# One exponent a head pair, queries and keys in a PSUM bank each, and new instruction orders in a fused attention and feed-forward kernel

## The chip, the cores and the metric

The kernel runs on one core of a Trainium2 chip. The metric is the device time of one execution in microseconds. The kernel before takes 2145.38 us, the median of three runs (2141.57 to 2145.68).

A core has TensorE (PE), which multiplies matrices and writes PSUM; VectorE (DVE) and ScalarE (ACT), which read PSUM and SBUF; GpSimd (POOL), which here works in SBUF alone; and SyncE (SP), whose queue issues all DMAs. Each engine takes its instructions strictly in the order of its own queue and waits for others by semaphores. PSUM has eight banks of 128 x 512 float32.

## The reference

Sixteen sequences of 512 tokens with 128 channels go through two stages.

```python
h = layernorm(x) * (1 + ca) + sa
x = x + ga * latent_attention(h)          # 16 heads of 8, causal
h = layernorm(x) * (1 + cb) + sb
x = x + gb * two_layers(h)                # DEPTH = 2
# one of the two layers:
h = shift_token(x); q, k, v = split(h @ wqkv)      # 8 heads of 64
q, k = l2norm(q) * q_scale, l2norm(k) * k_scale    # per token and head
q, k = rotary_xpos(q, k)                           # cos and sin factors
sim = mask(8 * q @ k.T)      # windows of 64 tokens, own and previous window
x = x + (softmax(sim) @ v) @ wo
h = layernorm(shift_token(x)) * lg + lb
x = x + (a * gelu(g)) @ w2 + b2, where a, g = split(h @ w1 + b1)
```

All arithmetic of the local attention is in float32.

## The kernel before

A batch is one sequence. A sequence of 512 tokens is four tiles of 128. For every batch `steps()` (line 56) lists the named steps: the first attention (`max`, `rows1`, `score`, `ctx`, `turn`, `join`, `out`, in four groups of four heads), then per layer four tiles of `qkv`, `rotate`, `v`, `norm`, `qheads`, `kheads`, four head pairs of `wscore`, `wexp`, `share`, `pturn`, `wctx`, then `wout`, the normalisation (`center`, `spread`, `scale`) and the feed-forward (`hid`, `down`). At the end comes `final`.

Two streams, the even and the odd batches, share the engines, each with buffers of its own (S2 = 2). The order of each engine is written out. `PLACES` says in which order an engine takes the steps of one batch, and `TURNS` has a bit for each step of the merged queue that says which stream is next (`merged`, line 144). Before the change both streams use one list. `FIRST_BANKS` (line 161) names the PSUM bank of every tile that PE writes; PE waits until the readers of the bank's last tile are done (`Banks.take`, line 221). `FILLS` (line 187) puts filler matmuls in front of chosen tiles (line 234); their results are overwritten.

The part that changes is the layers' attention:

- `qkv` (line 586): PE multiplies queries and keys of a tile into two adjoining banks, 128x1024. ScalarE squares all of it (788). `rotate`: VectorE multiplies it by the cosine factors (982) and, in two halves of every head, by the sine factors (989), and reduces the squares to sums a head (991). GpSimd adds the two products (1091).
- `norm`: ScalarE takes Ln and Exp of the sums (798, 800) for the inverse norms, GpSimd clips them (1096) and multiplies the keys by theirs (1101). The queries stay unscaled.
- `qheads`, `kheads`: PE turns the tile (430) and ScalarE copies it from PSUM (805). The queries' turn waits for GpSimd's sum, that of the keys for the product.
- `wscore`: PE writes the band mask and the scores of a pair of heads into two banks (627, 636). VectorE takes the negated maximum of each row (1000) and multiplies it by the inverse norm of the query (1006).
- `wexp` (815): for each head of the pair and each tile one ScalarE exponent of 128x128, with the inverse norm as scale, the maximum as bias and the row's sum from the accumulator. That is eight exponents a pair, and eight accumulator reads.
- `share`: VectorE takes the reciprocal of the sums (1021), GpSimd multiplies the probabilities by them (1108). `pturn`: PE turns them, VectorE copies them out of PSUM (1014). `wctx`: PE multiplies by the values (658), ScalarE copies (821).

Line 777 is the exponent of the first attention, 947 and 942 its maxima, 449 and 445 its scores and masks on PE, 928 the normalised input of the feed-forward and 678 its first product, 1033 the gated hidden rows, 741 the Exp of the normalisation, 1155 the store of a batch.

Of the kernel before, what the change touches and what calls it, by code (L numbers as in the profile page):

```python
# [54 lines left out]
def steps():  # L55
# [3 lines left out]
    out = [("keep",), ("values",)] + units[0] + [("rows1", 0)] + units[1] + [("rows1", 1)]  # L59
# [8 lines left out]
    for l in range(DEPTH):  # L68
        for t in range(NT + 2):
            out += [("qkv", l, t), ("rotate", l, t), ("v", l, t)] * (t < NT) + [("norm", l, t - 1)] * (1 <= t <= NT)  # L70
            out += [("qheads", l, t - 2), ("kheads", l, t - 2)] * (t >= 2)
        for p in range(NP2 + 2):
            out += [("wscore", l, p), ("wexp", l, p, 0), ("share", l, p, 0), ("wexp", l, p, 1), ("share", l, p, 1)] * (p < NP2)
# [4 lines left out]
    cut = out.index(("qkv", DEPTH - 1, 0)) + 1  # L78
    first = {("kheads", DEPTH - 1, 2): [("stats", 0)], ("kheads", DEPTH - 1, 3): [("plain", 0)],
             ("wscore", DEPTH - 1, 0): [("load",)], ("wscore", DEPTH - 1, 1): [("proj", 0), ("proj", 1)]}  # L80
    between = []
    for last in out[cut:]:
        between += [(1, last)] + [(0, name) for name in first.get(last, [])]
    return between + [(0, name) for name in out[:cut]]

# [14 lines left out]
    "ACT": [  # L100
# [141 lines left out]
def build(nc, x, wdkv, wuk, wuv, wuq, wo1, wqkv, q_scale, k_scale, wo, ln_g, ln_b, w1, b1, w2, b2,  # L242
          cond, wmod, c_f32, c_bits, c_rot, c_edge, out):
    with ExitStack() as ctx:
# [180 lines left out]
        with nc.Block() as block:  # L425
# [420 lines left out]
            def _(dve):  # L846
# [6 lines left out]
                def step(b, kind, *a):  # L853
# [115 lines left out]
                    elif kind == "rotate":  # L969
# [14 lines left out]
                        if n:  # L984
                            dve.wait_ge(*sum_r.at(b, n))
# [256 lines left out]
```

## Time and profile before

| | before |
|---|---|
| median of the runs | 2145.38 us |
| span of the profiled execution | 2140.7 us |
| PE busy | 1949.1 us, 91% |
| ACT busy | 1607.3 us, 75% |
| DVE busy | 1559.3 us, 73% |
| POOL busy | 862.1 us, 40% |
| mean granted clock of PE | 0.989 |

The profile is of one execution. Its own time is told by its span, from the first to the last instruction, 2140.7 us; the runs are timed from outside, so the median stands 4.7 us above it. "Busy" is time in which an engine had at least one instruction under way. The matmuls' ends are modelled, so a share of 91% is not 91% of the peak. A group of instructions is named by line, engine, operation and tiles; in the tiles' names `ps` is PSUM, `pr` and `scr` are work space, `Q` and `Kf` the turned queries and keys. "Idle before" is time in which the engine stood still ahead of such an instruction, with the engine and line that ended it.

### The profile page before, as it was taken

To read this page: it belongs to the slowest core of one execution; us is meant where nothing else is said; L and a number is where in the kernel's file an instruction comes from. 1 tells how busy PE (TensorE), PEld (TensorE's weight loads), DVE (VectorE), ACT (ScalarE), POOL (GpSimd) and SP (SyncE) were. 2 spreads that over 40 slices of the span, in tenths; PEclk is the share of its full clock that TensorE was granted. 3 is DMA by queue.
4 is the path that set the end of the run, shared out by engine and by line. 5 is a ranking of instruction groups with operands and counts; after the bars stand their busy time and mean duration, and the time that the engine had idled before them with its cause. 6 is when DMAs were issued, how large, how long until landed. Compare 5 with 4: busy or idle time off the path is not lost.

```text
span 2140.7 us, 56185 instructions
## 1 busy us (share of the span) xinstructions
PE 1949.1 (91%) x22308; PEld 1117.7 (52%) x22308; DVE 1559.3 (73%) x2671; ACT 1607.3 (75%) x3975; POOL 862.1 (40%) x826
## 2 busy tenths in 40 slices
PE   6789999999999999999999999999999999999987
PEld 3344545555454655545555554655545455554644
DVE  3476787877778777787877778687777877777753
ACT  1567878787887878777787887878688787877755
POOL 2043616245351624526163361625435162452522
PEclk8999999999999999999999999999999999999999
DMA  4110201213030120202112030120203012030100
GB/s 137 29 32 16 61 7 36 41 24 58 7 68 9 39 43 24 58 7 57 21 32 51 24 58 7 38 39 24 58 7 70 13 36 42 24 53 7 36 6 23
DMA packets 63110, 76.19 MB, mean 36 GB/s; under 512 B 10630, under 2 KB 57856, under 8 KB 60800
## 3 DMA queue, kind: packets, MB, share of 16 engines
q1 hardware_dynamic: 62852, 72.60, 16.1%
q8 instruction: 180, 2.95, 0.6%
q14 instruction: 78, 0.64, 0.1%
HBM read 9.14 MB, written 4.19 MB: 6 GB/s over the span
## 4 chain that ended last, share of the span: by engine, by line
PE 56%; ACT 23%; DVE 12%; issue 5%; SPq 2%; DMA 1%; POOL 1%; DVEq 0%; ACTq 0%; POOLq 0%
PE ps L430 10%; ACT pr L815 6%; PE ps L667 5%; PE ps L564 5%; ACT pr L777 5%; PE ps L594 4%; PE ps L595 4%; PE ps L604 4%; PE ps L658 3%; PE ps L449 3%; ACT pr L788 3%; DVE wm L1000 3%; PE ps L678 2%; PE ps L445 2%; PE ps L687 2%
## 5 line engine op out<-in xcount | busy, mean ns | idle before, releaser
L1091 POOL TENSOR_TENSOR pr<-pr 128x1024 f32<-128x1024 f32 x128 | 302.2, 2361 | 739.7 <-DVE pr L989 739.7
L815 ACT ACTIVATE pr<-ps,wb,inv 128x128 f32<-128x128 f32 x768 | 340.8, 481 | 24.6 <-DVE wb L1006 24.2
L777 ACT ACTIVATE pr<-ps 128x1024 f32<-128x1024 f32 x320 | 314.4, 1028 | 42.5 <-PE ps L449 42.0
L1108 POOL TENSOR_TENSOR pr<-pr,shares 128x512 f32<-128x512 f32 x192 | 199.9, 1048 | 314.0 <-DVE shares L1021 314.0
L947 DVE TENSOR_REDUCE nm<-ps 128x2 f32<-128x256 f32 (+2 forms) x384 | 314.5, 861 | 13.0 <-PE ps L449 11.9
L430 PE MATMUL ps<-cf,pr 128*128 128x128 f32 x1792 | 259.7, 282 | 31.1 <-POOL pr L1108 22.5
L430 PEld LDWEIGHTS ps<-cf,pr 128*128 128x128 f32 x1792 | 200.9, 142 | 124.4 <-issue 55.0
L982 DVE TENSOR_TENSOR pr<-ps,rot 128x1024 f32<-128x1024 f32 x128 | 156.2, 1221 | 120.1 <-ACT pr L788 97.7
L788 ACT ACTIVATE pr<-ps 128x1024 f32<-128x1024 f32 x128 | 131.2, 1025 | 104.6 <-PE ps L595 66.2
L445 PE MATMUL ps<-cb 64*64 64x256 bf16 (+1 forms) x2560 | 175.3, 263 | 30.1 <-ACT pr L777 14.4
L1014 DVE COPY pr<-ps 128x512 f32<-128x512 f32 x256 | 170.1, 679 | 15.2 <-PE ps L430 13.7
L815 ACT ACTIVATION_READ_ACCUMULATOR pr<-ps,wb,inv 128x1 f32 x768 | 175.9, 229 | 0.0
L1000 DVE TENSOR_REDUCE wm<-ps 128x8 f32<-128x1024 f32 x128 | 155.6, 1216 | 25.9 <-PE ps L636 25.9
L989 DVE TENSOR_TENSOR pr<-ps,rot 128x512 f32<-128x512 f32 x256 | 163.7, 681 | 0.0
L445 PEld LDWEIGHTS ps<-cb 64*64 64x64 bf16 x2560 | 72.4, 104 | 168.5 <-issue 82.7
L564 PE MATMUL ps<-pr,V 128*16 128x512 f32 (+3 forms) x2048 | 152.4, 439 | 6.3 <-ACT pr L777 6.3
L991 DVE TENSOR_REDUCE scr<-pr 128x16 f32<-128x1024 f32 x128 | 154.8, 1209 | 0.0
L594 PE MATMUL ps<-Wqkv,hs 128*128 128x512 f32 x256 | 137.1, 617 | 7.4 <-ACT pr L777 3.6
L1101 POOL TENSOR_TENSOR pr<-pr,inv 128x512 f32<-128x512 f32 x128 | 133.4, 1042 | 19.3 <-POOL inv L1096 0.4
L636 PE MATMUL ps<-Kf,Q 64*64 64x128 f32 (+1 forms) x4096 | 137.0, 263 | 0.0
L658 PE MATMUL ps<-pr 128*64 128x64 f32 x2048 | 133.4, 229 | 2.1 <-DVE pr L1014 1.9
L636 PEld LDWEIGHTS ps<-Kf,Q 64*64 64x64 f32 x4096 | 129.7, 133 | 4.5
(158 smaller groups left out, 4040.0 us busy)
## 6 DMA issues: line engine op xcount, KB each, us to landing
pr<-V SPq DMA_DIRECT2D x32, 512.0 KB, 4.5
queries<-early SPq DMA_DIRECT2D x224, 64.0 KB
keys<-early SPq DMA_DIRECT2D x224, 64.0 KB
pr<-V SPq DMA_DIRECT2D x32, 384.0 KB, 6.6
xn<-in_L_attn_x SPq DMA_DIRECT2D x16, 256.0 KB, 4.5
out<-hT SPq DMA_DIRECT2D x16, 256.0 KB, 2.2
queries<-mT SPq DMA_DIRECT2D x128, 4.0 KB
Wqkv<-in_L_ffn_wqkv SPq DMA_DIRECT2D x1, 1536.0 KB
```

What stands on the lines that cost most here:

```text
L430: mm = pe.transpose(dst[:, t * P:(t + 1) * P], src(t), ident)
L445: pe.matmul(dst, identb[here, here], mask, start=True, stop=False, skip_group_check=True)
L564: mm = pe.matmul(bank[32 * j:32 * j + 16, kt * P:T], V1[s][:, kt, 4 * g + j, :], pr[s][:, j, OFF[kt]:OFF[kt] + T - kt * P], start=(kt == 0 ...
L594: pe.matmul(bank[:, 0:T], lhs, Wqkv[:, l, 0:T], start=True, stop=True)
L636: mm = pe.matmul(bank[D2 * half:D2 * half + D2, r * T + (t + 1) * P - wd:r * T + (t + 1) * P], Q2[s][rows, p, q0:q0 + D2], K2[s][rows, p, ...
L658: mm = pe.matmul(bank[D2 * r:D2 * r + D2, q0:q0 + D2], val[s][:, t, 2 * p + r, :], PT[s][:, (2 * n + r) % 3, q0:q0 + D2], start=True, stop ...
L777: act.activation(dst, src, ACT.Exp, scale=SC1).then_inc(ex_r[s], 1)
L815: ins = act.activation(P2[s][2 * (p % 3) + r][:, o:o + P], bank[:, r * T + o:r * T + o + P], ACT.Exp, scale=inv[s][:, t, h:h + 1], bias=wb ...
L947: ins = dve.tensor_reduce(nm[s][:, qt, h:h + 2], src[:, :, o:o + (qt + 1) * P], AX_X, ALU.max, negate=True)
L1000: dve.tensor_reduce(dst, src, AX_X, ALU.max, negate=True).then_inc(wm_r[s], 1)
L1091: pool.tensor_tensor(t1[s][t % 3], t1[s][t % 3], t2[s], ALU.add).then_inc(sum_r[s], 1)
L1108: pool.tensor_tensor(part, part, share, ALU.mult).then_inc(part_r[s], 1)
```

## The change

- `qkv`, `rotate` become two steps a tile, queries (j = 0) and keys (j = 1), each with a bank of its own: two squares of 128x512, two cosine products of 128x512, four sine products of 128x256, two additions on GpSimd. The sum of squares stays one instruction.
- GpSimd multiplies the queries by their inverse norms too. `qheads` waits for that.
- `wscore`: VectorE takes the maxima and then adds the negated maximum to the scores, out of PSUM into SBUF (128x1024). The two banks are free after this.
- `wexp` is one exponent of 128x1024 in SBUF, in place, without scale, bias or accumulator. `share`: VectorE sums the rows (128x1024) and takes one reciprocal a pair. GpSimd's products stay two a pair.
- `pturn`: ScalarE makes the copy out of PSUM in place of VectorE.
- `PLACES`, `TURNS` and `FIRST_BANKS` are new. Each stream has a list of its own, and a stream may be up to three batches ahead in it. The first batch is in one list with the others, and the first attention's `stats`, `plain`, `load` and `proj` stand at the head of `steps()`. `FILLS` is empty.
- The SBUF tile `y` moves into `scr`, `P2` has three buffers of 128x1024 in place of six of 128x512.

```diff
-                        bank, full = banks.take(pe, (b, "qkv", l, t), [t_r.at(b, 3 * n)], 2)
+                        bank, full = banks.take(pe, (b, "qkv", l, t, j), [t_r.at(b, 3 * (2 * (n - 1) + j + 1))])
...
-                        pe.matmul(bank[:, 0:T], lhs, Wqkv[:, l, 0:T], start=True, stop=True)
-                        pe.matmul(bank[:, T:2 * T], lhs, Wqkv[:, l, T:2 * T], start=True, stop=True).then_inc(full, 1)
+                        pe.matmul(bank, lhs, Wqkv[:, l, j * T:(j + 1) * T], start=True, stop=True).then_inc(full, 1)
...
-                            pe.wait_ge(*sum_r.at(b, n))
+                            pe.wait_ge(*rot_r.at(b, 2 * n - 1))
...
-                        bank, full = banks.take(pe, (b, "wscore", l, p), [we_r.at(b, 2 * n + 2)], 2)
+                        bank, full = banks.take(pe, (b, "wscore", l, p), [wd_r.at(b, n + 1)], 2)
...
-                        act.activation(sqk[s], banks.wait(act, (b, "qkv", l, t)), ACT.Square).then_inc(sqk_r[s], 1)
+                        act.activation(sqk[s][:, j * T:(j + 1) * T], banks.wait(act, (b, "qkv", l, t, j)), ACT.Square).then_inc(sqk_r[s], 1)
...
                     elif kind == "wexp":
+                        l, p = a
+                        act.wait_ge(*wd_r.at(b, NP2 * l + p + 1))
+                        act.activation(P2[s][p % 3], P2[s][p % 3], ACT.Exp).then_inc(we_r[s], 1)
+                    elif kind == "pturn":
                         l, p, r = a
                         n = NP2 * l + p
-                        act.wait_ge(*wb_r.at(b, n + 1))
-                        bank = banks.wait(act, (b, "wscore", l, p))
-                        if p >= 3:
-                            banks.wait(act, (b, "pturn", l, p - 3, r))
-                        for t in range(NT):
-                            o, h = t * P, 2 * p + r
-                            ins = act.activation(P2[s][2 * (p % 3) + r][:, o:o + P], bank[:, r * T + o:r * T + o + P], ACT.Exp,
-                                                 scale=inv[s][:, t, h:h + 1], bias=wb2[s][:, t, h:h + 1],
-                                                 accum_out=sums[s][:, t, h:h + 1])
-                        ins.then_inc(we_r[s], 1)
+                        if 2 * p + r >= 3:
+                            banks.wait(act, (b, "pv", l, (2 * p + r - 3) // 2))
+                        bank = banks.wait(act, (b, "pturn", l, p, r))
+                        act.activation(PT[s][:, (2 * n + r) % 3, :], bank, ACT.Copy).then_inc(pt_r[s], 1)
...
-                        dst = wm2[s][:, :, 2 * p:2 * p + 2].rearrange("p t r -> p r t")
-                        dve.tensor_reduce(dst, src, AX_X, ALU.max, negate=True).then_inc(wm_r[s], 1)
+                        low = wm2[s][:, 2 * p:2 * p + 2, :].rearrange("p r t -> p (r t)")
+                        dve.tensor_reduce(low, src.rearrange("p (j n) -> p j n", n=P), AX_X, ALU.max, negate=True).then_inc(wm_r[s], 1)
...
+                        dve.tensor_tensor(P2[s][p % 3].rearrange("p (j n) -> p j n", n=P), src.rearrange("p (j n) -> p j n", n=P),
+                                          low.unsqueeze(2).broadcast_to([P, 2 * NT, P]), ALU.add).then_inc(wd_r[s], 1)
+                    elif kind == "share":
...
+                        dve.tensor_reduce(total, P2[s][p % 3].rearrange("p (j n) -> p j n", n=P), AX_X, ALU.add).then_inc(sum_w[s], 1)
...
-                        v = t1[s][t % 3][:, T:2 * T].rearrange("p (h d) -> p h d", d=D2)
-                        one = inv[s][:, t, H2:2 * H2].unsqueeze(2).broadcast_to([P, H2, D2])
-                        pool.tensor_tensor(v, v, one, ALU.mult).then_inc(rot_r[s], 1)
+                        for j in range(2):
+                            v = t1[s][t % 3][:, j * T:(j + 1) * T].rearrange("p (h d) -> p h d", d=D2)
+                            one = inv[s][:, t, j * H2:(j + 1) * H2].unsqueeze(2).broadcast_to([P, H2, D2])
+                            pool.tensor_tensor(v, v, one, ALU.mult).then_inc(rot_r[s], 1)
...
+FILLS = {}
```

## Rows read from the trace of the kernel before

**Rows 1.** Page, part 1: busy us, share of the span, instructions.

```profile
PE 1949.1 (91%) x22308; PEld 1117.7 (52%) x22308; DVE 1559.3 (73%) x2671; ACT 1607.3 (75%) x3975; POOL 862.1 (40%) x826
```

**Rows 2.** Timeline of SyncE's stores: start us, us, instruction.

```profile
441.71 0.39 SPq L1155 DMA_DIRECT2D out<-hT  x1
1963.52 0.40 SPq L1155 DMA_DIRECT2D out<-hT  x1
```

**Rows 3.** Windows: four of 264 us from 399 to 1455, summed.

```profile
sum 1056.00, PE 986.81 PEld 564.99 DVE 809.52 ACT 830.25 POOL 432.80; mean PE 246.70 PEld 141.25 DVE 202.38 ACT 207.56 POOL 108.20
```

**Rows 4.** Page, part 4: the chain that ended last, by engine.

```profile
PE 56%; ACT 23%; DVE 12%; issue 5%; SPq 2%; DMA 1%; POOL 1%; DVEq 0%; ACTq 0%; POOLq 0%
```

**Rows 5.** Waits of PE, 266 to 1862: us in total, times, longest.

```profile
PE ps L678 <- DVE y L928: 17.7, 12, 1.6
PE ps L430 <- POOL pr L1108: 13.6, 22, 0.9
PE ps L430 <- DVE pr L1014: 12.7, 12, 1.1
PE ps L445 <- ACT pr L777: 11.9, 26, 0.5
PE ps L627 <- DVE scr L1033: 6.1, 10, 0.7
```

**Rows 6.** L815 alone: windows summed over the run; its largest group.

```profile
sum 2141.00, ACT 461.31; mean ACT 230.65
L815 ACT ACTIVATE pr<-ps,wb,inv 128x128 f32<-128x128 f32 x768 | 340.8, 481 | 24.6 <-DVE wb L1006 24.2
```

**Rows 7.** Groups of ScalarE by form: busy us, mean ns, idle before.

```profile
L777 ACT ACTIVATE pr<-ps 128x1024 f32<-128x1024 f32 x320 | 314.4, 1028 | 42.5 <-PE ps L449 42.0
L805 ACT ACTIVATE Kf<-ps 128x512 f32<-128x512 f32 x128 | 73.5, 605 | 2.9 <-PE ps L430 2.9
L741 ACT ACTIVATE scr<-scr 128x512 f32<-128x512 f32 x32 | 20.2, 630 | 1.0
```

**Rows 8.** Groups of VectorE by form.

```profile
L982 DVE TENSOR_TENSOR pr<-ps,rot 128x1024 f32<-128x1024 f32 x128 | 156.2, 1221 | 120.1 <-ACT pr L788 97.7 <-issue 22.5
L989 DVE TENSOR_TENSOR pr<-ps,rot 128x512 f32<-128x512 f32 x256 | 163.7, 681 | 0.0
L991 DVE TENSOR_REDUCE scr<-pr 128x16 f32<-128x1024 f32 x128 | 154.8, 1209 | 0.0
L1014 DVE COPY pr<-ps 128x512 f32<-128x512 f32 x256 | 170.1, 679 | 15.2 <-PE ps L430 13.7
L1006 DVE TENSOR_TENSOR wb<-wm,inv 128x8 f32<-128x8 f32 x128 | 46.9, 367 | 4.4
L1021 DVE RECIPROCAL shares<-sums 128x4 f32<-128x4 f32 x256 | 42.4, 176 | 45.2 <-ACT pr L815 32.7 <-ACT scr L815 9.7 <-ACT y L815 0.7
L947 DVE TENSOR_REDUCE nm<-ps 128x2 f32<-128x256 f32 x128 | 53.4, 417 | 1.8 <-PE ps L449 1.2
```

**Rows 9.** Groups of GpSimd by form.

```profile
L1091 POOL TENSOR_TENSOR pr<-pr 128x1024 f32<-128x1024 f32 x128 | 302.2, 2361 | 739.7 <-DVE pr L989 739.7
L1108 POOL TENSOR_TENSOR pr<-pr,shares 128x512 f32<-128x512 f32 x192 | 199.9, 1048 | 314.0 <-DVE shares L1021 314.0
L1101 POOL TENSOR_TENSOR pr<-pr,inv 128x512 f32<-128x512 f32 x128 | 133.4, 1042 | 19.3 <-POOL inv L1096 0.4
```

**Rows 10.** Groups of PE: the filler matmuls.

```profile
L234 PE MATMUL ps<-cf 128*128 128x512 bf16 x161 | 48.5, 414 | 13.3 <-ACT Q L805 4.2 <-ACT V L791 3.1 <-DVE hT L1037 1.7
```

**Rows 11.** Windows: us, busy PE PEld DVE ACT POOL, granted clock, DMA, GB/s.

```profile
2070.00:2080.00 10.00, 6.08 (x18) 2.68 (x16) 7.68 (x9) 3.98 (x9) 4.96 (x3) 0.97 0.00 0
2080.00:2090.00 10.00, 8.77 (x28) 5.07 (x28) 6.51 (x8) 3.81 (x9) 8.58 (x8) 0.52 0.00 1
2100.00:2110.00 10.00, 8.01 (x96) 5.04 (x96) 6.92 (x16) 10.00 (x46) 5.80 (x6) 1.00 0.15 42
```

**Rows 12.** Window over one local softmax.

```profile
1095.70:1114.72 19.02, 16.13 (x224) 11.01 (x223) 15.76 (x36) 18.21 (x70) 6.20 (x6) 1.00 0.21 50
```

More of the change, by code:

```diff
@@ L77, in steps @@
     out += [("final",)]
[L78 to L84, printed above, removed]
-PLACES = {
[8 rows of a table removed]
-    "ACT": [
[6 rows of a table removed]
-    "DVE": [
[5 rows of a table removed]
-    "POOL": [
-        0, 3, 5, 7, 9, 15, 13, 18, 24, 28, 30, 35, 37, 42, 44, 50, 52, 32, 33, 70, 122, 130, 127, 135, 133, 137,
-        139, 145, 143, 148, 155, 157, 160, 162, 167, 169, 175, 177],
-    "SP": [
-        25, 31, 40, 48, 32, 33, 158, 165, 173, 76, 82, 93, 106, 68, 153, 125],
+    return out
@@ new lines @@
+PLACES = {
+    "PE": (
+        [
[8 rows of a table added]
+        [
[8 rows of a table added]
+    ),
+    "ACT": (
+        [
[7 rows of a table added]
+        [
[7 rows of a table added]
+    ),
+    "DVE": (
+        [
[4 rows of a table added]
+        [
[4 rows of a table added]
+    ),
+    "POOL": (
+        [
+            551, 554, 559, 197, 565, 200, 198, 252, 260, 262, 269, 265, 267, 275, 271, 273, 283, 279, 281, 286, 1,
+            293, 296, 301, 307, 324, 326, 333, 329, 331, 335, 337, 339, 347, 343, 345, 350],
+        [
+            454, 456, 463, 459, 461, 465, 467, 469, 477, 473, 475, 480, 487, 490, 495, 501, 518, 520, 527, 523, 525,
+            533, 529, 531, 541, 537, 539, 544, 195, 551, 554, 197, 559, 565, 198, 252, 200],
+    ),
+    "SP": (
+        [
+            355, 3, 4, 12, 18, 387, 29, 42, 61, 97],
+        [
+            255, 291, 355, 3, 4, 12, 18, 29, 42, 387],
+    ),
@@ L141 @@
+    "SP": (
+        "01bc60b7c60b7c60b7c60b7c60b7c60b7c60b7db"),
 }
 def merged(engine):
-    names = [steps()[i] for i in PLACES[engine]]
-    rest = [iter([(b, name) for k in range(B // S2 + 1) for back, name in names for b in [s + S2 * (k - back)] if 0 <= b < B])
-            for s in range(S2)]
+    names = steps()
+    rest = [iter([(b, names[i % len(names)]) for k in range(B // S2 + 4) for i in PLACES[engine][s]
+                  for b in [s + S2 * (k - i // len(names))] if 0 <= b < B]) for s in range(S2)]
@@ L286, in build @@
         hs = [sb(f"hs{s}", [P, T]) for s in range(S2)]
-        y = [sb(f"y{s}", [P, T]) for s in range(S2)]
         Q = [sb(f"Q{s}", [P, NP2 * T]) for s in range(S2)]
@@ L304, in build @@
         inv = [sb(f"inv{s}", [P, NT, 2 * H2]) for s in range(S2)]
-        wm2 = [sb(f"wm2{s}", [P, NT, H2]) for s in range(S2)]
-        wb2 = [sb(f"wb2{s}", [P, NT, H2]) for s in range(S2)]
+        wm2 = [sb(f"wm2{s}", [P, H2, NT]) for s in range(S2)]
         rec = [sb(f"rec{s}", [P, NT, 4])[:, :, :] for s in range(S2)]
@@ L328, in build @@
         ctx2 = [a[:, 0:4 * T].rearrange("p (h n) -> p h n", n=T) for a in scr]
-        sums = [sb(f"sums{s}", [P, NT, H2]) for s in range(S2)]
-        shares = [sb(f"shares{s}", [P, NT, H2]) for s in range(S2)]
+        sums = [sb(f"sums{s}", [P, H2, NT]) for s in range(S2)]
+        shares = [sb(f"shares{s}", [P, H2, NT]) for s in range(S2)]
         hid = [a[:, 0:3 * T].rearrange("p (c n) -> p c n", n=T) for a in scr]
@@ L969, in step @@
                     elif kind == "rotate":
-                        l, t = a
+                        l, t, j = a
                         n = NT * l + t
                         i = t % 3
-                        bank = banks.wait(dve, (b, "qkv", l, t))
-                        dve.wait_ge(*sqk_r.at(b, n + 1))
+                        bank = banks.wait(dve, (b, "qkv", l, t, j))
+                        dve.wait_ge(*sqk_r.at(b, 2 * n + j + 1))
                         if n == 0 and b < S2:
@@ L1006, in step @@
[L1006 to L1021 removed]
+                        if p >= 3:
+                            for r in range(2):
+                                banks.wait(dve, (b, "pturn", l, p - 3, r))
```

198 lines of the change are left out of this document (97 added, 101 removed), and 62 rows, old and new, of tables (FILLS, PLACES).

## The prediction

> **What bounds the kernel now.** I read the busy totals first. TensorE is at work for 1949.1 of 2140.7 us, ScalarE for 1607.3, VectorE for 1559.3 and GpSimd for 862.1 [rows 1]. Then the rhythm: the stores of batches 1 and 13 start at 441.71 and 1963.52 [rows 2], so a batch takes (1963.52 − 441.71)/12 = 126.8 us, and what stands outside 13 such periods (filling and draining the pipeline) is 2140.7 − 13 × 126.8 = 492.3 us. Over eight and a third periods in the middle, 1056 us [rows 3], the engines' busy time scaled to one period is PE 986.81/1056 × 126.8 = 118.5, ACT 99.7, DVE 97.2 and POOL 52.0 us. PE is thus the bound, but no single engine explains the whole: it is idle 8.3 us a period. The chain of waits says the same in shares: PE 56%, ACT 23%, DVE 12% [rows 4]. TensorE's work is fixed by this change, so what can be won is its idle time and a few filler matmuls, and nothing else.
>
> Who makes PE wait is in its waits between 266 and 1862 us, 12.6 periods [rows 5]. The five longest are the normalised input of the feed-forward (17.7), the scaled probabilities from GpSimd (13.6), the copy of the turned probabilities by VectorE (12.7), ScalarE's early exponents, which hold PSUM (11.9), and the gated hidden rows (6.1). The listed ones come to 62.0 us; 8.3 × 12.6 = 105 us is the idle time in all.
>
> **ScalarE, part by part.** All exponents of the local attention with their accumulator reads fill 461.3 us [rows 6]. That view takes overlapping records once; the mean of 481 ns for one in the groups runs into its accumulator read and may not be added to it. The change puts in 128 exponents of 128x1024. The early attention's exponent of that shape takes 1.028 us from PSUM, and a 128x512 exponent from SBUF takes 0.630 where a 128x512 copy from PSUM takes 0.605 [rows 7], so reading SBUF costs a few hundredths more: 128 × 1.03 = 132 us, at most 128 × 1.26 = 161 (two halves of 0.63). It takes over 256 copies of 128x512: 256 × 0.605 = 155 us. The square is cut in two: 256 × 0.605 − 128 × 1.028 = +23 us. Net 461 − 132 − 155 − 23 = 151 us less, 9.4 a batch: 99.7 goes to 90.3 us a period.
>
> On the source of the exponent the Trainium skill (VectorE: DVE Perf Modes, errata-adjusted cycle table) gives ScalarE 52 cycles more from SBUF than from PSUM. An estimate from that page is 128 × 0.043 = 6 us over the run, off the path; the rows above agree in sign (0.630 against 0.605).
>
> **VectorE.** Added: 128 subtractions out of PSUM, like today's cosine product of 128x1024 (156.2 us in 128), and 128 sums of 128x1024 out of SBUF, like today's sum of squares (154.8). Removed: 256 copies (170.1), the 128 small products (46.9), and half the reciprocals (42.4 − 128 × 0.18 = 19). Cutting the cosine product in halves costs 256 × 0.68 − 156.2 = +18 [rows 8]. For the sine products of 128x256 there is no row of that operation. 128x1024 takes 1.22 and 128x512 takes 0.68, so a fixed 0.14 us and 0.27 for 256 elements make 0.41, near the reduction over 256 at 0.417: 512 × 0.41 − 163.7 = +46, with 0 as the other end. The sum is +139 us, 8.7 a batch: 97.2 goes to 106 us a period, 84% of the present one.
>
> The Trainium skill (VectorE: DVE Perf Modes, rules for kernel authors) speaks against this move: a tensor_reduce on the hot path runs at 1x only and should be restructured away. The trace agrees: 1.209 us for 1024 columns and 0.417 us for 256 [rows 8], a slope of 1.03 ns a column, which is 1x of 0.96 GHz on that page. So the row sums really cost what I enter.
>
> **GpSimd.** It now scales the queries too, 128 × 1.042 = +133 us; its additions, cut in two, cost 256 × 1.05 instead of 302.2, −33 [rows 9]. That is +6 a batch on an engine at 52 of 126.8: hidden by its own idle time. What is no longer hidden is delay: the turns of the queries now wait for sum, Ln, Exp, clip and product, where they waited for one addition. The turns of the keys wait for that chain today, and a window's scores need both, so I cost it at 0; exposed, it is one product of 1.04 us per layer and batch, 33 us.
>
> **Banks.** A pair of heads holds two of eight banks today from the maximum until the last of eight small exponents: 1.22 + 0.37 + 461.3/128 = 5.2 us, queues aside. Afterwards it holds them for the maximum and the subtraction, 2.4 us. Over eight pairs that is 2 × 8 × 2.8 = 45 bank-us of 8 × 126.8 = 1014. Queries and keys in a bank each free a bank after half the work. This works against the waits on held banks (11.9) and lets scores run ahead. The added wait of the exponent for the subtraction queues the early exponents and copies behind it on ScalarE, which has 36 us of slack a period.
>
> **Orders.** Reading the order tables in sequence, the streams keep about the same lag. What differs is slack: between the second window score of layer 1 and the first turn of its pair there are 5 other TensorE steps today and 10 afterwards. In the last stage, input normalisation to hidden rows, the distance stays about the same. I take it that the three waits that the change reaches (13.6 + 12.7 + 11.9 = 38.2 us in 12.6 periods, 3.0 each) go, and that the others stay; the bounds are +5 and −8.3 a period. What is late next are the row sums, then the feed-forward's normalisation.
>
> **Fillers and clock.** The fillers are 161 matmuls, 48.5 us [rows 10]. Those in mid-run stand in waits: 0. At the end they sit between the steps of the last softmax, where the granted clock stayed at 1.00 (2.4 GHz). Twenty us before, after 10 us of which PE was busy for 6.1, it was 0.52 (near the 1.2 GHz level) for 10 us [rows 11], with PE busy 8.8 of them; at full clock half of that work would do, so about 4 us were lost. Without fillers this happens once more: +4 us, between 0 and 15 (most of the last 25 us at half speed). At the start the first maxima wait for the spreading transfers; I enter 0.
>
> **Sum.** 2140.7 − 13 × 3.0 + 4 = 2105.7 us. The median of the runs is 2145.38, 4.7 over the span of the profiled execution; with that, 2110 us.
>
> **Rivals.** (1) The new order removes most of TensorE's other waits as well. For it speaks that ScalarE falls to 90 and that both streams get an order of their own; against it, that feed-forward and last turns are chains with little beside them. At three quarters of the idle time: 6.2 × 13 = 81 us, 2140.7 − 81 + 4 + 4.7 = 2068 us. The limit is 8.3 × 13 = 108, 2041 us.
> (2) VectorE takes ScalarE's place in the softmax, and the kernel is slower. Between 1095.7 and 1114.7 ScalarE is busy 18.2 and VectorE 15.8 of 19.0 us [rows 12]. The edit adds 4 × (1.22 + 1.21) − 8 × 0.664 − 4 × 0.37 − 4 × 0.18 = 2.2 us there, which still fits with 1.0 to spare. It decides where VectorE, in order, reaches a sum before its exponent is done: 1.03 plus a hand-over of some 0.2, for half of the eight pairs 4.9 us a batch, against 3.0 gained. 13 × 1.9 + 4 = 29: 2174 us. Other steps stand between a score and its sum in the new tables, which speaks against it.
> (3) Each removed wait is replaced by one as long, since ScalarE's and VectorE's work together stays at 197 us a period (196 after): 2145 to 2149 us.
>
> **How the numbers follow.** Main case 47%, rival (1) 15%, rival (2) 28%, rival (3) 10%. About 0.2% is what a measurement here can tell from nothing. Faster is the main case and (1), 62%; of (3) most is within it, 7%; the rest, 31%, is slower. The range runs from 2045, near the limit of (1), to 2178, just past (2); the main case by itself is 2080 to 2135.
>
> **What would show it.** Stores 123.8 us apart. ScalarE near 1456 us and VectorE near 1698. TensorE's waits for the scaled and turned probabilities nearly gone. The exponents near 1.03 us and the sums near 1.21. A stretch at a clock of 0.5 among the last 40 us. It is wrong if VectorE idles before its sums for the exponents, or if the distance of the stores is 126.8 or more.

## The result: slower by 3.2%, and the profile after

| | before | after |
|---|---|---|
| median of the runs | 2144.48 us (4 runs) | 2212.39 us (4 runs, 2209.26 to 2216.56) |
| ratio | | 1.0316, 95% interval 1.0301 to 1.0332 |
| span of the profiled execution | 2140.7 us | 2214.8 us |
| mean granted clock of PE | 0.989 | 0.971 |

The forecast was 2110 us, range 2045 to 2178. The time lies outside, on the other side of no change.

The same rows of the changed kernel as [rows 1]:

```profile
span 2214.8 us, 54780 instructions
PE 1975.5 (89%) x22147; PEld 1117.7 (50%) x22147; DVE 1681.9 (76%) x2799; ACT 1454.5 (66%) x2455; POOL 1003.6 (45%) x1082
```

The work moved as forecast: ScalarE 1454.5 us (1456 forecast), VectorE 1681.9 (1698). The groups of the changed kernel, by form (busy us, mean ns, idle before), against [rows 7 to 9]:

```profile
L839 ACT ACTIVATE pr<-pr 128x1024 f32<-128x1024 f32 x96 | 101.5, 1057 | 29.9 <-DVE pr L1033 29.6
L846 ACT ACTIVATE pr<-ps 128x512 f32<-128x512 f32 x256 | 147.0, 595 | 102.1 <-PE ps L461 82.8 <-PE ps L688 18.1
L1033 DVE TENSOR_TENSOR pr<-ps,wm 128x1024 f32<-128x1024 f32 x96 | 117.5, 1224 | 3.3
L1042 DVE TENSOR_REDUCE sums<-pr 128x8 f32<-128x1024 f32 x96 | 116.2, 1211 | 24.3 <-ACT pr L839 24.3
L1016 DVE TENSOR_TENSOR pr<-ps,rot 128x256 f32<-128x256 f32 x512 | 191.1, 415 | 7.8 <-POOL pr L1117 7.8
L1117 POOL TENSOR_TENSOR pr<-pr 128x512 f32<-128x512 f32 x256 | 321.7, 1274 | 603.6 <-DVE pr L1016 602.7
```

In the changed kernel 839 is the exponent of a head pair, 846 the copy of a turned pair, 1033 the subtraction, 1042 the sum, 1016 a sine product and 1117 GpSimd's addition. The exponent takes 1.057 us, the sum 1.211, the sine product 0.415 (0.41 estimated). SyncE's stores of batches 0, 1, 8, 9, 10 and 13 after the change:

```profile
313.95 0.40 SPq L1183 DMA_DIRECT2D out<-hT  x1
457.17 0.39 SPq L1183 DMA_DIRECT2D out<-hT  x1
1355.63 0.40 SPq L1183 DMA_DIRECT2D out<-hT  x1
1501.12 0.40 SPq L1183 DMA_DIRECT2D out<-hT  x1
1617.96 0.40 SPq L1183 DMA_DIRECT2D out<-hT  x1
2022.34 0.40 SPq L1183 DMA_DIRECT2D out<-hT  x1
```

From batch 1 to 13 it is (2022.34 − 457.17)/12 = 130.4 us a batch against 126.8 [rows 2], +43.4 us. Batch 1 is 15.5 us later, and from batch 13 to the end it is 192.5 us against 177.2, +15.3. The sum, 74 us, is the difference of the spans. The stores also come in turns of 143 to 145 and 117 us: the two streams no longer stand half a pair apart. The store of batch 0 starts at 313.95 us against 314.64 before, so the 15.5 us up to batch 1 all arise between the first two stores, 143.2 us apart instead of 127.1.

What the steady stretch consists of (window over it, columns as in [rows 12], first before, then after):

```profile
441.71:1963.52 1521.81, 1421.87 (x16628) 820.21 (x16632) 1160.83 (x1981) 1204.80 (x2976) 644.91 (x613) 1.00 0.17 35
```

```profile
457.17:2022.34 1565.17, 1449.36 (x16573) 818.76 (x16572) 1251.06 (x2068) 1090.19 (x1835) 747.44 (x800) 0.98 0.16 34
```

PE is busy 27.5 us longer at the same work, even without the 60 fillers that stood in this stretch, and idle 115.8 us instead of 99.9, +15.9. I cut the stretch into windows of 2.5 us and added up 2.5 × (1 − granted clock): 3.4 us before, 27.3 after. So most of the added busy time is the same work at a lowered clock. Within one pair of batches, slices of 10 us in which TensorE idles most or its clock is low, and the one ahead of them:

```profile
1385.63:1395.63 10.00, 9.75 (x112) 6.72 (x110) 7.72 (x10) 4.84 (x9) 3.37 (x5) 1.00 0.01 2
1395.63:1405.63 10.00, 5.96 (x112) 4.24 (x113) 9.73 (x22) 5.88 (x10) 4.69 (x5) 1.00 0.62 146
1405.63:1415.63 10.00, 9.71 (x43) 5.11 (x38) 7.43 (x13) 5.31 (x11) 6.99 (x8) 0.83 0.26 67
1445.63:1455.63 10.00, 6.50 (x98) 4.78 (x97) 7.68 (x11) 9.89 (x11) 3.11 (x5) 0.89 0.09 20
1525.63:1535.63 10.00, 7.32 (x81) 4.33 (x74) 9.80 (x22) 7.04 (x12) 3.41 (x4) 1.00 0.13 28
1575.63:1585.63 10.00, 6.82 (x99) 5.12 (x98) 8.27 (x10) 8.09 (x11) 5.81 (x7) 0.88 0.37 79
```

There are two kinds. At 1395 and 1525, layer 1's softmax, VectorE is full (9.73 and 9.80 of 10). At 1445, layer 0's softmax, ScalarE is full (9.89); at 1575, layer 0's softmax too, it has 8.09 beside a VectorE at 8.27. In or right behind three of the four the clock falls (0.83, 0.89, 0.88). The waits of PE, 300 to 1900 (us in total, times, longest), go against [rows 5]. Here 461 is the turn (430 before), 476 a mask of the first attention (445), 688 the product with the values (658), 1136 GpSimd's scaled probabilities (1108), 1128 its product for queries and keys, 860 Gelu and 807 the early exponent (777):

```profile
PE ps L476 <- ACT pr L846: 19.1, 6, 3.2
PE ps L688 <- DMA pr<-V: 11.9, 6, 3.5
PE ps L461 <- ACT pr L846: 11.5, 6, 1.9
PE ps L461 <- POOL pr L1136: 11.5, 24, 1.0
PE ps L461 <- ACT scr L860: 8.1, 6, 1.4
...
PE ps L461 <- POOL pr L1128: 5.2, 19, 0.4
...
PE ps L476 <- ACT pr L807: 1.1, 6, 0.2
```

The wait for PSUM held by the early exponents (L807) is down from 11.9 to 1.1, that for the scaled probabilities only from 13.6 to 11.5. The wait for the copy of the turned pairs (12.7) is gone from VectorE, but it went over to ScalarE with the copy: 11.5 us ahead of turns and 19.1 ahead of masks of the first attention, 6 times each and up to 3.2 us long. New are also the waits for Gelu (8.1), for the shifted values' transfer (11.9) and for the product that now scales the queries too (5.2). ScalarE in a layer 0 softmax, where it also has the other stream's Gelus of layer 1:

```profile
1182.51 1.06 ACT L839 ACTIVATE pr<-pr 128x1024 f32<-128x1024 f32 x1
1183.59 1.28 ACT L860 ACT_TABLE_LOAD   x1
1184.88 0.69 ACT L860 ACTIVATE scr<-ps,B 128x512 f32<-128x512 f32 x1
1185.59 1.28 ACT L839 ACT_TABLE_LOAD   x1
1186.88 1.06 ACT L839 ACTIVATE scr<-scr 128x1024 f32<-128x1024 f32 x1
1187.84 1.06 ACT L846 ACTIVATE pr<-ps 128x512 f32<-128x512 f32 x2
1188.93 1.28 ACT L860 ACT_TABLE_LOAD   x1
```

One stream's exponents alternate with the other's Gelus, and each change of function costs a load of 1.28 us. Of the 9.7 us from 1182.51 to 1192.20 four loads take 5.1 (the fourth starts at 1190.92). The copies of turned pairs stand in the same queue: the turn that starts at 1188.98 had waited 1.92 us for one. In all there are 44 such extra loads after, 28 before. The Trainium skill (ScalarE: Activation LUTs, What ACT_TABLE_LOAD costs) adds a drain of some 1380 ns to each load, 2.66 us a switch. This trace does not agree: the exponent of 1182.51 ends at 1183.57, the load starts at 1183.59, and Gelu follows at 1184.88, so a switch costs 1.3 us.

### The profile page after: what moved, and what is told of

It reads as the page before. It is cut to its first block and busy times, and to the rows that moved or that the text cites. A ratio compares the mean times of both kernels' runs of the same rounds, so it can differ in the third digit from the quotient of the medians.

```text
span 2214.8 us, 54780 instructions
## 1 busy us (share of the span) xinstructions
PE 1975.5 (89%) x22147; PEld 1117.7 (50%) x22147; DVE 1681.9 (76%) x2799; ACT 1454.5 (66%) x2455; POOL 1003.6 (45%) x1082
## 3 DMA queue, kind: packets, MB, share of 16 engines
q1 hardware_dynamic: 62852, 72.60, 15.5%
## 5 line engine op out<-in xcount | busy, mean ns | idle before, releaser
L1117 POOL TENSOR_TENSOR pr<-pr 128x512 f32<-128x512 f32 x256 | 321.7, 1274 | 603.6 <-DVE pr L1016 602.7
L461 PE MATMUL ps<-cf,pr 128*128 128x128 f32 x1792 | 274.2, 289 | 72.4 <-POOL pr L1136 22.0
L807 ACT ACTIVATE pr<-ps 128x1024 f32<-128x1024 f32 x320 | 309.5, 1028 | 20.1 <-PE ps L595 13.9
L625 PE MATMUL ps<-Wqkv,hs 128*128 128x512 f32 x512 | 257.0, 617 | 22.2 <-DVE hs L952 12.0
L1128 POOL TENSOR_TENSOR pr<-pr,inv 128x512 f32<-128x512 f32 x256 | 261.5, 1043 | 19.3 <-POOL inv L1122 0.4
L846 ACT ACTIVATE pr<-ps 128x512 f32<-128x512 f32 x256 | 147.0, 595 | 102.1 <-PE ps L461 82.8
L1016 DVE TENSOR_TENSOR pr<-ps,rot 128x256 f32<-128x256 f32 x512 | 191.1, 415 | 7.8 <-POOL pr L1117 7.8
L818 ACT ACTIVATE pr<-ps 128x512 f32<-128x512 f32 x256 | 148.7, 591 | 62.9 <-PE ps L625 39.8
L688 PEld LDWEIGHTS ps<-pr 128*64 128x64 f32 x2048 | 117.1, 148 | 73.5 <-issue 54.4
L625 PEld LDWEIGHTS ps<-Wqkv,hs 128*128 128x128 f32 x512 | 86.4, 192 | 108.1 <-issue 65.2
L688 PE MATMUL ps<-pr,V 128*64 128x64 f32 x2048 | 139.9, 234 | 0.0
```

The lines of the kernel that those rows point to most:

```text
L461: mm = pe.transpose(dst[:, t * P:(t + 1) * P], src(t), ident)
L625: pe.matmul(bank, lhs, Wqkv[:, l, j * T:(j + 1) * T], start=True, stop=True).then_inc(full, 1)
L688: mm = pe.matmul(bank[D2 * r:D2 * r + D2, q0:q0 + D2], val[s][:, t, 2 * p + r, :], PT[s][:, (2 * n + r) % 3, q0:q0 + D2], start=True, stop ...
L807: act.activation(dst, src, ACT.Exp, scale=SC1).then_inc(ex_r[s], 1)
L1016: dve.tensor_tensor(t2[s][:, own].rearrange("p (h d) -> p h d", h=H2)[:, :, o:o + 32], qk[:, :, q:q + 32], sin, ALU.mult).then_inc(t_r[s], 1)
L1117: pool.tensor_tensor(t1[s][t % 3][:, own], t1[s][t % 3][:, own], t2[s][:, own], ALU.add).then_inc(sum_r[s], 1)
```

## The experiments

All ratios are to the kernel before on the same chip, by 3 rounds. Over the chips used its median lay between 2144.5 and 2147.2 us, so differences of 3 us or less between two rows say nothing. "After" is the changed kernel, 2212.4 us.

| kernel | median us | ratio, 95% interval |
|---|---|---|
| all three changes on the orders of before | 2414.1 | 1.1252 (1.1236 to 1.1269) |
| softmax alone | 2525.6 | 1.1775 (1.1757 to 1.1793) |
| bank split alone | 2121.0 | 0.9888 (0.9873 to 0.9902) |
| copies alone | 2311.2 | 1.0773 (1.0755 to 1.0791) |
| after, Gelus together | 2203.2 | 1.0267 (1.0251 to 1.0282) |
| after, no table loads | 2164.7 | 1.0085 (1.0068 to 1.0102) |
| before, no table loads | 2133.2 | 0.9942 (0.9928 to 0.9957) |
| after, no sums | 2196.0 | 1.0231 (1.0209 to 1.0253) |
| after with the fillers | 2203.8 | 1.0262 (1.0245 to 1.0279) |
| before without fillers | 2157.4 | 1.0054 (1.0037 to 1.0070) |
| bank split, exponent behind the Gelus | 2160.4 | 1.0067 (1.0052 to 1.0082) |
| after, copies on VectorE | 2355.3 | 1.0972 (1.0956 to 1.0988) |
| after, values earlier | 2218.4 | 1.0341 (1.0326 to 1.0357) |
| after, input's transfer behind | 2292.1 | 1.0685 (1.0669 to 1.0700) |
| after, 8 fillers in the transfer's wait | 2207.5 | 1.0284 (1.0267 to 1.0301) |
| after, exponents ahead of the Gelus | 2216.8 | 1.0336 (1.0320 to 1.0351) |
| after, no table loads, no sums | 2133.4 | 0.9940 (0.9925 to 0.9955) |
| after, three edits that gained | 2198.8 | 1.0243 (1.0226 to 1.0260) |

**The parts on the orders of before.** My first theory was that the new computation is harmless and the new order tables cost the time; the rival, that the computation does. The bank split:

```diff
-bank, full = banks.take(pe, (b, "qkv", l, t), [t_r.at(b, 3 * n)], 2)
+for j in range(2):
+    bank, full = banks.take(pe, (b, "qkv", l, t, j), [t_r.at(b, 3 * (2 * (n - 1) + j + 1))], at=...)
```

> The kernel before with queries and keys in a bank each and nothing else: four squares and rotations of 128x512 more for each 128x1024 one. By the rows of before and after VectorE gets 24 us and ScalarE 15 us more over the kernel, mostly beside TensorE. Theories A and C: 2135 to 2155. Theory B has VectorE's fixed costs count where it is already full: 2150 to 2170.

It gained 24 us, more than any theory had: the stores are 125.6 us apart. So this part of the change is good, and it makes the one version here that does the whole computation and beats both kernels. These waits of TensorE in the kernel before, between the stores of batches 1 and 13, are not in the list of the split kernel:

```profile
PE ps L504 <- DVE pr L989: 4.8, 12, 0.4
PE ps L594 <- ACT pr L777: 2.7, 12, 0.2
PE ps L594 <- ACT hs L839: 2.3, 12, 0.2
```

The first is a projection of the first attention that waited for VectorE's sine product, the others the product for queries and keys. The wait for the early exponents' banks stays (11.0 before, 10.9 with the split). The other parts:

```diff
+dve.tensor_tensor(P2[s][p % 3]..., src..., low..., ALU.add)          # softmax alone: subtraction,
+act.activation(P2[s][p % 3], P2[s][p % 3], ACT.Exp)                  # one exponent,
+dve.tensor_reduce(total, P2[s][p % 3]..., AX_X, ALU.add)             # sum; queries normalised too
```

> The kernel before with the new softmax alone (subtraction and sums on VectorE, one exponent of 128x1024 a head pair, queries and keys normalised on GpSimd); the copies of the turned pairs stay on VectorE, queries and keys share a pair of banks, the orders are those of before. Theory A: 2130 to 2165. Theory B: VectorE holds the copies too (some 75 us more than after), so this is the slowest of the four, 2210 to 2260. Theory C: 2130 to 2165, like A, but then the kernel with the copies alone is over 2180.

```diff
-dve.tensor_copy(PT[s][:, (2 * n + r) % 3, :], bank)                  # copies alone
+act.activation(PT[s][:, (2 * n + r) % 3, :], bank, ACT.Copy)
```

> The kernel before with the copies of the turned pairs (256 of 128x512) on ScalarE and nothing else: ScalarE 152 us more on top of 1607 (1760), VectorE some 170 us less. The softmax of before had ScalarE at 18.2 of 19.0 us in layer 1, so all theories have this slower: A 2170 to 2200, from the 16 exponents of 0.48 us, not from the copies as such; B 2150 to 2190; C over 2190, with TensorE waiting over 20 us for the copies.

> The kernel before with its own orders, banks and fillers, but with all three changes of the computation: subtraction on VectorE and one exponent for a head pair, both query and key normalised on GpSimd, queries and keys in a bank each, turned-pair copies on ScalarE (placed between its steps by where their banks fill). Theory A (the loss of 67 us comes from the new order tables: ScalarE's exponents and Gelus of the two streams alternate and TensorE waits 3 to 4 us with its clock down after it, twice a pair of batches): within 20 us of 2144, 2125 to 2165. Theory B (the loss lies in the new operations: VectorE does 123 us more and ends the softmax, whatever the order): 2195 to 2240, with VectorE over 97% busy in the layer-1 softmax and TensorE waiting there for it over 4 us more a batch. Theory C (the copies in ScalarE's queue): slow here and in the kernel with the copies alone, and not in the one with the softmax alone.

+380, +166 and +268 us: far above every range with an upper end. The copies alone fit only theory C's open "over 2190", and not its mechanism: from 300 to 1900 TensorE waits 13 us for copies, where C had over 20, and 53 us for the eight exponents a pair that share ScalarE with them, as A had it. C also had the softmax alone as fast as before, and falls with that. In the kernel with the softmax alone TensorE's group of transposes tells where (idle before and its releasers at the end):

```profile
L430 PE MATMUL ps<-cf,pr 128*128 128x128 f32 x1792 | 293.1, 297 | 247.3 <-POOL pr L1097 150.4 <-POOL pr L1105 72.9 <-DVE nm L938 18.8
```

L1097 is GpSimd's product that now normalises the queries as well. TensorE meets their turns at the old place, where they waited for one addition only. L1105 is its product for the probabilities. These runs thus don't measure the new softmax by itself; they show that it can't run on the old order, and that the new tables win back some 200 of 268 us. My first theory fell in the form in which I had put it.

**Table loads.** Gelu became an identity of the same shape, and the preloads went, in both kernels:

```diff
-act.preload_act_table_set(GELU)
-act.activation(gel[s][0:cn_, c % 2, :], bank[0:cn_, :], ACT.Gelu, bias=...)
+act.activation(gel[s][0:cn_, c % 2, :], bank[0:cn_, :], ACT.Identity, bias=...)
```

> The changed kernel with no table loads at all inside the loop: Gelu is left out of the computation (the activation is the identity with its bias, of the same shape), and with it its preloads. 108 loads of 1283 ns go from ScalarE (139 us of 1454). Theory A: at least 60 us less than 2212, 2100 to 2150, and less than 25 us from the same edit of the kernel before. Theory B: 2185 to 2205, the difference to the same edit of the kernel before stays 60 us or more.

> The kernel before with the same left out (Gelu is the identity, no table loads in the loop): 92 loads of 1283 ns go from ScalarE (118 us of 1607). Its loads stand mostly where ScalarE is not last; theories A and B both: 2100 to 2140.

Without loads the changed kernel gains 48 us and the old one 11 to 13. Theory A (60 or more) and B (60 left between the kernels) both missed. Of the 68 us between them 31.5 are left, so 36 come from table loads: all 108 in the one against all 92 in the other, the extra ones and those around every group of Gelus. With them go 25.6 of the 27.3 us that the lowered clock took in the steady stretch (1.7 left). The waits for the copies in ScalarE's queue go with the loads, from 11.5 and 19.1 us to this one line, while the wait for the scaled probabilities grows from 11.5 to 21.8:

```profile
PE ps L476 <- ACT pr L846: 6.6, 6, 1.1
```

Can the loads be had back in a kernel that keeps Gelu? Two regroupings of ScalarE's order:

```diff
+mine = [(b, ("hid", 1, c)) for c in range(3)]            # for each batch, in ScalarE's order:
+i = order.index(mine[0]) + 1
+order[i:i] = mine[1:]                                     # the other two behind the first
```

> The changed kernel with one thing moved: layer 1's three Gelu steps of a batch follow each other in ScalarE's order, so that no exponent of the other stream stands between them and some 36 of its 44 extra table loads (1283 ns each, 46 us of ScalarE in all) go. Queries and keys in a bank each have been measured at 24 us less on the order of before, so 91 us are to be explained. Theory A (the loss is the table loads and the stalls with a lowered clock behind them): 2150 to 2190. Theory B (VectorE's share of the softmax, subtraction and sum in its queue, is what is late): 2203 to 2215. Theory D (the third Gelu moved ahead now waits for its bank and holds up the exponents behind it): 2215 to 2235.

```diff
+mine = [step for step in order[first:last] if step[1][0] == "wexp"]   # between hid 0 and hid 2
+order[first:first] = mine                                             # now ahead of hid 0
```

> The changed kernel with the layer 0 exponents that stood between the three Gelus of the other stream moved ahead of them: the same table loads go as with the Gelus together (9 us gained, the wait moved to GpSimd's scaling). Theory A: the exponents are on the chain and the Gelus are not, 2170 to 2195. Rival: the Gelus become the late ones (their banks and the product after them), 2200 to 2225.

The first gained 9 us, the second nothing. All 44 extra loads went in both, but a wait came for them. In the second it is the Gelus that are late, as the rival said: TensorE waits 23.6 us for them, 6 times, up to 3.9. In the first, ScalarE itself and then VectorE stand still, in layer 0's softmax:

```profile
1435.74 0.68 ACT L872 ACTIVATE scr<-ps,B 85x512 f32<-85x512 f32 x1 [2.54 <-DVE scr L1070]
1438.83 1.22 DVE L1054 TENSOR_REDUCE sums<-pr 128x8 f32<-128x1024 f32 x1 [2.52 <-ACT pr L851]
```

and what TensorE does meanwhile:

```profile
1441.55 2.08 PE L473 MATMUL ps<-cf,pr 128*128 128x128 f32 x8 [3.87 <-POOL pr L1148]
```

The first line is the third Gelu. Its result goes into the buffer of the first one (there are two, `c % 2`), and VectorE frees that buffer only with its product of the gated rows (1070), which stands behind its own softmax work. ScalarE waits 2.54 us for it here, as long as two of the loads that were saved, and 15.2 us in 6 such places from 300 to 1900. VectorE then stands 2.52 us before a sum whose exponent is queued behind the Gelus, and TensorE 3.87 us for what GpSimd makes of that sum. Theory D had such a stall, with a bank as its cause. A third buffer, or an earlier product on VectorE, is the obvious next try; no run has it. The same lesson from the other side, on the bank split, where one exponent of the early attention went behind the third Gelu of layer 0:

> The kernel before with queries and keys in a bank each (measured 2121) and, in ScalarE's order, the exponent that stood between the second and third Gelu of layer 0 moved behind the third: 28 table loads of 1283 ns go (36 us of ScalarE). With all loads gone the kernel before gained 12 us. Theory A (loads cost where ScalarE is last): 2112 to 2119. Rival: the moved exponent is now late for TensorE by a Gelu, 2121 to 2130.

This is 28 loads less and 39 us more than with the split alone, past both forecasts: TensorE waits 22.7 us in the stretch 300 to 1900 for that exponent, 12 times. There the alternation was the cheaper order.

**VectorE's sums.** Left out, with a small copy in their place:

```diff
-dve.tensor_reduce(total, P2[s][p % 3]..., AX_X, ALU.add)
+dve.tensor_copy(total, wm2[s][:, 2 * p:2 * p + 2, :]...)
```

> The changed kernel with the sum of the exponents left out: VectorE copies 128x8 values of the maxima in its place, so 128 sums of 1.21 us go and 128 copies of some 0.15 us come (135 us of 1682 on VectorE; the probabilities are scaled wrongly). Everything waits for the same semaphores. Theory A: 2195 to 2212, VectorE is late in the layer-1 softmax only, by 0.8 us a time. Theory B: under 2170, because the sum stands behind other work in VectorE's queue in every head pair and all of its 1.2 us lie on the chain.

> The changed kernel with Gelu left out (identity, no table loads) and the sums of the exponents left out (a copy of 128x8 in their place). Apart they gained 48 and 16 us. Theory F (two limits one behind the other, in different stretches: loads in layer 0's softmax, VectorE in layer 1's): at least their sum, 64 us, 2120 to 2148. Theory G (VectorE is no limit once the loads are gone, the rest is the orders and the uneven distance of the two streams): 2150 to 2160.

Alone it gained 16 us; with the table loads gone it gained 31 (2164.7 to 2133.4). Together the two edits gain 79 us, more than the 64 of each by itself, as theory F had it, and the changed kernel then stands where the old one stands without loads (2133.2). The stores come 125.1 us apart instead of 126.9. The two limits partly hide each other; that they lie in different stretches is read from the slices above. The Trainium skill (VectorE: DVE Perf Modes, rules for kernel authors) says of a tensor_reduce on the hot path that it is the slowest operation of that engine, and to consider restructuring it. The gain agrees with the advice: 31 us for 128 sums that became copies of 0.26 us. "Slowest" this trace does not show: the subtraction of the same shape takes 1.224 us, the sum 1.211.

**The wait for the values' transfer, and fillers.**

```diff
+for t in (3, 2):                       # odd batches, in the orders of PE and ACT
+    order.remove((b, ("v", 1, t)))
+    order.insert(order.index((b, ("v", 1, 1))) + 1, (b, ("v", 1, t)))
```

> The changed kernel with layer 1's last two value products of odd batches (TensorE), and their copies (ScalarE), moved right behind the second one, some 4 us earlier, so that the shifted values' transfer starts earlier and the exponent of the second head pair no longer stands behind the last copy (it stood 2.8 us after its subtraction had ended). 7 places. Theory A2 (this order is what costs: 1.7 to 3.5 us of waiting and 1.7 us of half clock, 3.4 to 5.2 us a place): 2176 to 2190. Rival (VectorE sets the pace there, 9.7 us of 10 busy): TensorE waits as long for the sums instead, 2203 to 2213.

The same two windows as above, here as 1394.54 and 1404.54, and the one of layer 0:

```profile
1394.54:1404.54 10.00, 8.19 (x125) 5.41 (x126) 9.76 (x23) 5.21 (x9) 4.08 (x4) 1.00 0.57 134
1404.54:1414.54 10.00, 8.64 (x58) 4.49 (x58) 9.93 (x18) 6.58 (x13) 9.04 (x10) 1.00 0.30 52
1444.54:1454.54 10.00, 6.49 (x68) 4.58 (x57) 8.20 (x12) 9.64 (x12) 4.55 (x5) 0.75 0.00 0
```

The wait for the transfer (11.9 us) has left the list, PE is busy 8.19 instead of 5.96 us in the first window and keeps its clock in both, and nothing is gained: the kernel takes 6 us more, 5 past the rival's range. In TensorE's list (300 to 1900) other waits grew by nearly as much: for the scaled probabilities from 11.5 to 15.3 us, for VectorE's input to the product of queries and keys from 8.1 to 10.8, for the subtraction ahead of a turn from 3.8 to 6.4. At layer 0 the clock is low for longer (0.75 against 0.89). VectorE is full there (9.76 and 9.93 of 10) and these waits end with it or with GpSimd behind it, as the rival had it.

```diff
-FILLS = {}
+FILLS = {354: 8, 660: 8, 966: 8, ...}   # first product with the values, odd batches
```

> The changed kernel with 8 filling matmuls (some 1.7 us at full clock) in odd batches at layer 1's first product with the values, where TensorE waits for their transfer; nothing else, no work goes or moves. If half of the harm of this wait is the clock behind it (three slices a pair of batches at 0.83 to 0.89): 7 times 1.7 us, 2197 to 2205. If the clock falls for what comes later: 2209 to 2216.

```diff
+order.remove((b, ("out",)))            # even batches, in SyncE's order
+order.insert(order.index((b + 1, ("proj", 1))) + 1, (b, ("out",)))
```

> The changed kernel with one transfer moved: the next input's 256 KB go behind the projections' 28 transfers on SyncE's queue instead of right behind the shifted values (odd batches). The values took 8.2 us to land there and 4.4 to 5.6 elsewhere. If the collision is what delays them: waits for the transfer go from 12 us to under 4 over the stretch 300 to 1900, 2195 to 2205. If it isn't: 2208 to 2214.

The 8 fillers gave 5 us, between the two forecasts and barely outside the spread: its runs are 2203.5 to 2211.6 us, those of after 2209.3 to 2216.6. The moved transfer cost 80, which no theory had: ScalarE then waited up to 13 us at a time for that input's statistics, with the turned keys of the other stream queued behind (PE's waits of that kernel):

```profile
PE ps L670 <- ACT Kf L848: 76.7, 11, 12.3
```

The wait for the values' transfer stayed as it was, 12.5 us against 11.9 in 6 waits each, though the input's transfer is now issued some 40 us behind it. So the input is not what delays the values; what does stays open. The fillers of the kernel before, put back and taken away:

> The changed kernel has an empty table of fillers; this one gets the 161 filling matmuls of before back, at the steps of the same names (20 of them at the first maximum, where TensorE idles 14.8 us at the start; 4 and 1 at layer 1's first two turned pairs of each batch). Read from the traces: at full clock there is 27 us less in the twelve periods of after that the lowered clock takes (before 3 us), and 38 against 20 us at both ends. Theory E (the missing fillers let the clock fall): 2165 to 2190. Theory A (the clock falls because of stalls that the fillers don't cover; the fillers of a period stand elsewhere): 2205 to 2215 or slower by what the fillers take, up to 16 us (75 of 0.21 us); only the start gains, some 5 us.

> The kernel before with its table of fillers emptied and nothing else. Theory E: 2170 to 2200, most of the 67 us. Theory A: 2145 to 2162; a few us at the start and the end, and at layer 1's softmax, where 5 fillers of a batch cover a wait of VectorE for 1 to 2 us.

They are worth 9 us in the one and 10 in the other; theory E fell. Most of it lies at the ends: in its profiled execution, the slowest of its four runs, the kernel before without fillers reaches its second store 8.6 us later and needs 184.6 instead of 177.2 us behind the store of batch 13, while its stores are 127.1 us apart instead of 126.8.

**Copies back on VectorE, and what gained put together.**

> The changed kernel with the 256 copies of turned pairs on VectorE, placed between its steps by where their banks fill: ScalarE gets 152 us less, VectorE some 175 us more (1682 to 1857 of 2212). Theory C (the copies in ScalarE's queue are what TensorE waits for, 30 us in the stretch from 300 to 1900): 2185 to 2205. Theory B (VectorE is full in the softmax): 2250 to 2300. Theory A (the copies are late through the table loads ahead of them alone): no gain from moving them, 2220 to 2280 since VectorE is now busier.

> The changed kernel with layer 1's Gelus together (9 us gained alone), the fillers of before (9 us) and 8 fillers in the transfer's wait of odd batches (5 us). If they add up: 2187 to 2193. If the fillers covered the same clock losses as the other edits: 2193 to 2203. In no case below the kernel before.

The copies on VectorE cost 143 us more, 55 past theory B's range: VectorE has no room for them beside subtraction and sum, as B had it. They were put into an order that was made without them, so the size is not that of the copies alone; that VectorE is what TensorE then waits for, up to 4.0 us at a time, is in its trace. The three edits together gave 14 us, not 23; they cover the same losses in part.

## Why the prediction was wrong

- **Engine totals: right but for GpSimd, ScalarE's partly by luck.** ScalarE was 1.5 us off, VectorE 16. In ScalarE's total 16 more table loads (20.5 us) were not entered, and three items came out lower: the copies 147 us for 155, the squares 17.5 more for 23, the early exponents 309.5 for 314.4. GpSimd got 141 us instead of 100: an addition of 128x512 takes 1.274 us, where 1.05 was entered, which is the time of a product with a broadcast factor (1.048, [rows 9]). The delay of the queries' turns behind that product was entered at 0. TensorE's waits for the product come to 20.7 us over the whole kernel, 1.6 before: 5.2 from 300 to 1900, 6.4 in the first 300 us and 8.5 behind the store of batch 13, up to 3.9 at once. So it is nearly hidden in the middle and exposed at the two ends.
- **The step that failed is Orders: "the three waits that the change reaches go, and the others stay", −3.0 us a period.** Measured is +3.6 a period. Of the three only the one for the early exponents went (11.9 to 1.1). The one for the scaled probabilities shrank by 2 us, and the one for the copy moved to ScalarE with the copy and grew, from 12.7 to 11.5 and 19.1 us. I had entered nothing for new waits. I had read the tables for the distance between a score and its turn on TensorE, and not for what stands between two exponents or copies on ScalarE. The table loads, some 1.28 us at each change of function, are in the trace of before (28 extra ones there); they stood in no term of my sum. They make 36 of the 68 us, and without them the waits for the copies fall to 6.6 us.
- **Rival (2) had the mechanism of most of the rest, too small.** The sums on VectorE cost 16 us with the loads in place and 31 without; the rival had 29. That the two numbers are close is partly luck: the rival counted VectorE's idle time before a sum, 4.9 us a batch, which came out at 24.3 us in all or 1.5 a batch (the row above), while the runs without sums price the 1.21 us of the sums themselves. That a full VectorE passes a delay of ScalarE on through GpSimd to TensorE is seen at one place above; how much it costs in all no run tells. With 28% for it and the range ending just past its 2174, I allowed for it alone, and not for it with another.
- **Fillers: +4 was too small**, 9 to 10 us measured, mostly at start and end. I entered 0 for the start, where 20 of them stood.
- **Banks: too small, and the wrong wait.** I set the split against the wait on the early exponents' banks, which it left at 10.9 us. What went were three other waits, 9.8 us in twelve periods, and the two short falls of the clock (3.4 us); alone the split is worth 24 us.
- **The clock in mid-run was not in the sum.** The clock falls behind the few waits of 1.9 to 3.5 us, and not behind those of before, 1.6 us at most [rows 5]: 27.3 us against 3.4, while the idle time as such grew by 15.9 only.

Not settled: with loads and sums out the two kernels are level, yet the new one has the split (−24 on the old order) and no fillers (+10). If these effects add up, which is not shown, some 14 us stay with the subtraction, the copies or the orders. No run separates them, since the old order can't carry the new softmax. The longer way to batch 1 is the first long interval of the uneven streams (143.2 us for 127.1), but what sets that distance is open. Behind the store of batch 13, 15.3 us longer, the rows show two things beside the missing fillers, and no run takes them apart: TensorE's 8.5 us of waits for the queries' and keys' product (1.2 before), and 18.9 us of 2.5 × (1 − granted clock) against 5.1.

## What to carry to other kernels

A shorter chain is not enough. One head pair's way from the scores to its shares got shorter by the instructions' own times, from 5.4 us (maximum 1.22, small product 0.37, exponents 3.6, reciprocal 0.18) to 4.9 (1.22, subtraction 1.22, exponent 1.06, sum 1.21, reciprocal 0.20), and the kernel got slower: what counts is what else stands in the queues, which two streams share. Before trusting a reordered ScalarE queue, count the changes between functions of different tables and look at what each Gelu or exponent holds up; removing the loads by grouping can cost more than it gives, and a grouped step needs its buffer free at the new place. A change of several parts is best timed part by part: the smallest part here, a bank each for queries and keys, gains 1.1% on the old orders.

## What the runs showed of the hardware

- A table load took 1283 ns on ScalarE each time that Exp and Gelu alternated, whether preloaded or not (all 109 loads of the changed kernel).
- After the change the granted clock fell to 0.50 to 0.53 (the 1.2 GHz level) for some 3 us during or right behind each of the five places between the stores of batches 7 and 11 where TensorE had waited over 1.9 us at once (3.18, 3.49, 1.91, 3.18 and 1.92 us), and behind none of the others, 1.65 us at most. It is no rule for every kernel: the kernel before fell to 0.62 at 1484.9 with no single wait over 1.1 us near it, and with loads and sums left out a wait of 1.72 us was followed by 0.56. With the wait of 3.49 us filled or gone the clock stayed at 1.00 there; in the kernel with the values earlier it was low for longer behind the next one (0.75 over 10 us against 0.89), and the sum over the steady stretch went only from 27.3 to 25.6 us, with the fillers to 23.9.
- An addition of 128x512 on GpSimd took 1.274 us where a product with a broadcast factor took 1.043; one of 128x1024 took 2.361.
